# Routing and scattering of an expert layer's rows inside the attention before it, and results scattered by tags

## The chip, the cores and the metric

The kernel runs on one core of a Trainium2 chip. Its five engines are TensorE (PE), VectorE (DVE), ScalarE (ACT), GpSimd (POOL) and SyncE (SP); each works through its own list of instructions in order and waits for semaphores that others raise. DMAs are issued from SP's, ACT's and POOL's lists. The metric is the device time of one execution in microseconds; of several runs, the median counts.

## The reference

Two transformer blocks over 8 sequences of 256 tokens with 256 values (2,048 tokens). What matters here is the second block: an attention with 16 query heads and 4 key/value heads, causal, and behind it a mixture of experts.

```python
x = x + _L1_attn_ref(_layernorm(x), ...)
x = x + _L1_ffn_ref(_layernorm(x), ...)

# _L1_ffn_ref: 32 experts, 4 for each token, inner width 128, and a shared expert
logits = flat @ router_w.T
scores = jnp.sqrt(jax.nn.softplus(logits))
_, idx = jax.lax.top_k(scores + expert_bias, K)
topv = jnp.take_along_axis(scores, idx, axis=1)
topv = topv / (topv.sum(axis=-1, keepdims=True) + 1e-20)
probs = jnp.zeros((T, E), flat.dtype).at[jnp.arange(T)[:, None], idx].set(topv)
# for each expert: acc + p[:, None] * _clamped_swiglu(flat, wg, wu, wd)
out = out + _clamped_swiglu(flat, shared_gate_w, shared_up_w, shared_down_w)
```

## The kernel before

All engines' programs are written out by hand, with their waits. The stages follow each other: a front (projections of the first block), attention(0), a middle (output projection, the first block's expert choice, projections of the second block), attention(1), routing, shared expert, expert loop, combination.

**Attention.** `attention(n)` runs over 8 sequences b and 16 heads s. TensorE computes the scores twice: `pair` gives them to DVE, which takes the row maxima (L1423 in the second attention, six reduces a sequence), and `scores` gives them, with the maxima subtracted, to ACT for the exponential (L775). The maxima travel as two more rows of the stacked queries: DVE writes `neg`, TensorE turns it (`turn_maxima`, at head 8), ACT copies it to `negT` (L754, at head 9), and `stack_maxima` (L596, on POOL's list) sends two small DMAs into the rows of qs; TensorE waits for them at the start of the sequence (`neg_stacked`). In the second attention the stacked queries and keys come from DRAM by 12 DMAs for each 512 tokens that SP issues (`stack_middle`, L447 and L450). `values` multiplies four heads' probabilities with v; `turn_back` and `divide` (head 5 of the next sequence) give the normalized context, and DVE adds it to x (L1453).

Scores for ACT, maxima and turned values share a ring of three PSUM banks, `st_bank`. Its uses are listed in order in `RING_USES`; `wait_ring` makes TensorE wait until the use three places earlier is read.

**Routing**, all tokens at once after attention(1), with 16 tiles of 128 tokens: statistics (L1510 to L1517, ACT takes the root), normalized rows `xn4` (L1519), transposes (L1132) and copies (L1524), 64 matmul records for the logits (L1138), softplus as Exp and Ln and a square root on ACT (L813 to L817), the four best (L1542, L1545), one-hot `pick` (L1548) and its sum `chosen` (L1553), the weights `pk[1]` (L1556 to L1561), then with matmuls of ones and a triangle the rank of every row in its expert (L1147 to L1151), the table of blocks of 128 rows (L1565 to L1595), and the row numbers `slot` (L1581). Experts lie one behind the other, each rounded up to blocks, so that a row's place depends on the counts of all tokens.

**Scatter and loop.** POOL scatters each of 16 x 4 columns of rows into `rows_by_expert` (L647, 128 rows of 1 KB each). Meanwhile the shared expert runs in four chunks of 512 tokens (TensorE L1161, L1173; DVE L1602 to L1613; ACT L820). SP loads all experts' weights once attention(1) is over (L542), and the first blocks after the last scatter (L544). The loop works on 80 blocks here, four in each round, in a pipeline: TensorE turns the rows (L1193), computes gate and up (L1206), turns the hidden values (L1215), goes down (L1221); DVE clips (L1618), copies (L1637) and multiplies (L1624, L1630); ACT copies, takes tanh, copies the result (L837) and stores it to `results_by_expert` (L839).

**Combination.** When all results are stored (L1658), POOL gathers 64 times 128 rows by `slot` into eight buffers (L654), and DVE adds each, times its weight, to x (L1666). SP stores x, two tiles at a time (L559).

Both DRAM tables are filled with zeros before (L515, L516; 96 blocks and the last 32), by SP during attention(0).

## Time and profile before

| | us |
|---|---|
| runs (3) | 832.95, 834.35, 834.79; median 834.35 |
| profiled execution | 840.46 |
| its span, first to last instruction | 836.2 |
| mean granted TensorE clock | 0.832 |

| engine | busy us | share of the span |
|---|---|---|
| PE | 567.1 | 68% |
| DVE | 452.4 | 54% |
| ACT | 312.0 | 37% |
| POOL | 194.7 | 23% |

The page cuts the span into 40 slices of 20.9 us and gives the busy tenths of each. TensorE is at 7 to 9 in the first half and in the expert loop; between slice 20 and 27, and after the loop, it stands nearly still. Busy times are measured for each instruction; "idle before" is the time in which the engine stood in front of it, with who released it. "issue" as a releaser means that the profile shows nothing that was waited for. The granted clock is 1.00 at 2.4 GHz and 0.50 at 1.2 GHz.

### The profile page before, as it was taken

The numbers are of one execution on the slowest core, as the hardware profiler recorded it, in microseconds if no ns is written. First come the engines' busy times: TensorE is split into PE (matmuls) and PEld (weight loads), VectorE is DVE, ScalarE is ACT, GpSimd is POOL, SyncE is SP. The second block draws the span as 40 slices with busy tenths as digits, with TensorE's granted clock in tenths as the row PEclk, the third lists the DMA queues.
The fourth block names the chain that finished last, engine by engine and source line by source line (L and its number), as shares of the span: only waits on it lengthen the run. The fifth ranks groups of instructions, "written<-read, shape, count | busy, mean of one in ns | idle before, by whom it ended". The sixth has DMA issues, their size and how long they took to land.

```text
span 836.2 us, 13730 instructions
## 1 busy us (share of the span) xinstructions
PE 567.1 (68%) x4179; PEld 395.1 (47%) x4181; DVE 452.4 (54%) x1088; ACT 312.0 (37%) x755; POOL 194.7 (23%) x227
## 2 busy tenths in 40 slices
PE   5985797897977987999966235501799999960000
PEld 2652364454864556777746213200576767740000
DVE  4656487571688554666636595110455555543333
ACT  2441466566545523556650200000344455430000
POOL 2340000004110430000000017776000000007775
PEclk9995899899989897999995566755899999995555
DMA  6889949900000588000029202222344444423443
GB/s 197 224 264 215 204 152 408 351 2 3 1 2 0 148 255 184 3 4 3 3 71 421 114 6 94 106 101 103 101 136 134 137 135 134 138 84 118 129 140 114
DMA packets 61933, 107.40 MB, mean 128 GB/s; under 512 B 9333, under 2 KB 47421, under 8 KB 60477
## 3 DMA queue, kind: packets, MB, share of 16 engines
q1 hardware_dynamic: 43196, 79.23, 30.9%
q0 software_dynamic: 7168, 17.05, 6.5%
q10 hardware_dynamic: 11520, 10.49, 3.7%
q8 instruction: 29, 0.48, 0.2%
q14 instruction: 20, 0.16, 0.1%
HBM read 58.38 MB, written 47.97 MB: 127 GB/s over the span
## 4 chain that ended last, share of the span: by engine, by line
PE 48%; DVE 17%; issue 11%; POOL 8%; DMA 8%; ACT 4%; another core or an unknown queue 3%; SPq 1%; ACTq 0%; POOLq 0%; DVEq 0%
PE banks L1206 8%; POOL arena L654 6%; PE banks L1045 6%; PE banks L1221 5%; DMA arena<-negT 5%; PE banks L1007 4%; PE banks L884 4%; DVE mx L1420 3%; PE banks L1066 2%; PE banks L1193 2%; PE banks L1215 2%; PE banks L1048 2%; PE banks L890 2%; PE banks L952 2%
## 5 line engine op out<-in xcount | busy, mean ns | idle before, releaser
L775 ACT ACTIVATE arena<-banks 128x512 f32<-128x512 f32 (+1 forms) x256 | 130.8, 549 | 105.5 <-PE banks L1045 54.9
L1045 PE MATMUL banks<-arena 98*128 98x256 bf16 (+1 forms) x512 | 95.1, 274 | 30.5 <-DMA arena<-negT 22.7
L654 POOL DMA_INDIRECT arena<-results_by_expert,bpb x64 | 60.7, 948 | 187.9 <-DVE hold L1658 168.7
L1420 DVE TENSOR_REDUCE mx<-banks 128x4 f32<-128x1024 f32 x64 | 76.3, 1221 | 40.2 <-PE banks L1007 40.1
L1007 PE MATMUL banks<-arena 96*128 96x256 bf16 (+1 forms) x512 | 89.6, 282 | 5.2 <-DVE mx L1420 3.8
L647 POOL DMA_INDIRECT rows_by_expert<-arena,bpb x64 | 63.8, 997 | 99.1 <-DVE bpb L1581 79.9
L1206 PE MATMUL banks<-arena,attn_w 128*128 x320 | 83.8, 385 | 4.0 <-ACT attn_w L824 3.3
L1423 DVE TENSOR_REDUCE mx<-banks 128x4 f32<-128x1024 f32 (+1 forms) x48 | 58.3, 1223 | 40.1 <-PE banks L1011 39.4
L1045 PEld LDWEIGHTS banks<-arena 98*128 98x128 bf16 x512 | 47.3, 102 | 67.0 <-DMA arena<-negT 24.5
L601 POOL DMA_DIRECT2D arena<-negT x32 | 15.8, 497 | 230.0 <-ACT negT L754 230.0
L1007 PEld LDWEIGHTS banks<-arena 96*128 96x128 bf16 x512 | 53.1, 106 | 22.5 <-DVE mx L1420 7.3
L824 ACT ACTIVATE attn_w<-banks 128x256 f32<-128x256 f32 x80 | 30.6, 383 | 80.4 <-ACT attn_w L837 27.9
L1618 DVE TENSOR_SCALAR attn_w<-banks 128x256 f32<-128x256 f32 x80 | 34.0, 424 | 47.6 <-PE banks L1206 47.4
L1206 PEld LDWEIGHTS banks<-arena,attn_w 128*128 128x128 f32 x320 | 55.3, 193 | 9.1 <-issue 4.8
L1666 DVE SCALAR_TENSOR_TENSOR arena<-arena,pk 128x256 f32<-128x256 f32 x64 | 31.0, 485 | 51.4 <-DMA arena<-results_by_expert,bpb 47.0
L1221 PE MATMUL banks<-arena,attn_w 128*128 x160 | 51.5, 404 | 0.6
L1173 PE MATMUL banks<-arena 128*128 128x256 f32 x32 | 13.3, 588 | 51.2 <-DVE arena L1608 44.2
L1193 PE MATMUL banks<-ident,pvs 128*128 128x128 f32 x160 | 31.2, 279 | 18.2 <-DMA pvs<-rows_by_expert 18.2
L1011 PE MATMUL banks<-mask_s,identb 128*128 128x128 bf16 x256 | 43.1, 230 | 0.0
L1048 PE MATMUL banks<-mask_t,identb 128*128 128x128 bf16 x256 | 42.0, 224 | 0.0
L1066 PE MATMUL banks<-arena 128*17 128x256 f32 x512 | 36.3, 404 | 1.1 <-ACT pvs L763 1.1
L1173 PEld LDWEIGHTS banks<-arena 128*128 128x128 f32 x32 | 9.0, 295 | 56.3 <-DVE arena L1608 45.8
(197 smaller groups left out, 1024.3 us busy)
## 6 DMA issues: line engine op xcount, KB each, us to landing
arena<-parts_dram SPq DMA_DIRECT2D x72, 256.0 KB, 7.0
rows_by_expert<-zero SPq DMA_DIRECT2D x1, 12288.0 KB, 40.5
arena<-in SPq DMA_DIRECT2D x1, 12288.0 KB, 32.6
pvs<-rows_by_expert SPq DMA_DIRECT2D x80, 128.0 KB
results_by_expert<-attn_w ACTq DMA_DIRECT2D x80, 128.0 KB, 2.0
parts_dram<-arena SPq DMA_DIRECT2D x24, 384.0 KB, 3.2
results_by_expert<-zero SPq DMA_DIRECT2D x1, 4096.0 KB, 49.5
arena<-in SPq DMA_DIRECT2D x4, 512.0 KB, 6.6
```

The costliest lines, as they stand in the source:

```text
L647: pool.indirect_dma_start(xs, bass.IndirectOffsetOnAxis(ap=slot[:, t, k:k + 1], axis=0), xn4[:, t, :], None).then_inc(scattered, 16)
L654: pool.indirect_dma_start(yg[:, n % YG, :], None, ys, bass.IndirectOffsetOnAxis(ap=slot[:, t, k:k + 1], axis=0)).then_inc(gathered[n % YG] ...
L775: act.activation(pt[:, i % P_RING, 0:width], st_bank[RING_AT["s", b, s] % 3][:, 0:width], ACT.Exp, scale=HD ** -0.5).then_inc(exp_ready[n], 1)
L1007: ins = pe.matmul(dst[:, a * nk:(a + 1) * nk], q_rows(n, slice(0, STACK), h0 + a, b, qt * P, P), k_rows(n, slice(0, STACK), h0 + a, b, 0, ...
L1045: ins = pe.matmul(dst[:, at:at + SEQ - q0], keys, q_rows(n, slice(0, ROWS), s, b, q0, SEQ - q0), start=True, stop=(n == 0))
L1048: ins = pe.matmul(dst[:, at:at + P], identb[:, :], mask_t[:, :], start=False, stop=True)
L1066: ins = pe.matmul(pv_bank[rows, col:col + SEQ], vals, p[:, kt * SEQ:(kt + 1) * SEQ], start=(kt == 0), stop=(kt == QT - 1))
L1193: ins = pe.transpose(bank[p][:, k * P:(k + 1) * P], xb[:, q, k * P:(k + 1) * P], ident[:, :])
L1206: ins = pe.matmul(bank[2 + p][:, 0:2 * INNER], xbT[:, p, k, :], experts[:, bass.ds(e * EW + k * 2 * INNER, 2 * INNER)], start=(k == 0), st ...
L1221: pe.matmul(bank[6 + p][:, 0:D], hidT[:, p, :], experts[:, bass.ds(e * EW + 2 * KD * INNER, D)], start=True, stop=True).then_inc(y_ready, 1)
L1420: ins = dve.tensor_reduce(out, src.rearrange("p (q h k) -> p q h k", q=QT, k=nk), AX.X, ALU.max)
L1423: ins = dve.tensor_reduce(out, src.rearrange("p (h k) -> p h k", k=nk), AX.X, ALU.max)
```

## The change

**Layout.** `rows_by_expert` gets room for all 2,048 tokens in each expert (`EXPERTS * TOKENS` rows), so that a row's place is expert x 2,048 + rank and doesn't depend on later tokens. Rows become 260 values: 256 and four tags, expert x 16,384 + the number of the (token, choice) pair. Only the first 128 rows of each expert are cleared. A block may begin anywhere (`start_i`); an expert's last block is moved back to end with its rows, and rows that were done in the block before go to a trash area.

**Routing in the attention.** After `divide` of a sequence DVE takes its statistics; POOL takes the inverse root (`ALU.pow`) and ACT normalizes the rows at heads 8 and 10 of the next sequence; TensorE turns them at head 12 into a bank of the ring, and ACT copies. For five batches of sequences (3, 2, 1, 1, 1) logits are computed at head 14, ACT does Exp and Ln at head 15, POOL takes the square root as a power (`root`), DVE finds the best four and picks them at heads 3 and 8 of the second sequence after the batch, TensorE computes the ranks there at head 10 and DVE the row numbers at head 11. POOL scatters a batch's columns as soon as it has them, in between its small operations. Batches 3 and 4 end after the attention.

**Moved.** `stack_maxima(1, b)` goes from POOL to SP, behind `stack_middle(3)`. SP loads the experts in four parts, 5, 5 and 6 experts when their memory becomes free during the attention, and 16 when all slots are known; the shared expert's weights come after the last division. The weights `pk[1]` are computed after the expert loop.

**Expert loop.** ACT no longer stores. DVE finds for each block, from the tags, where its rows belong, and POOL scatters the result to the place of its (token, choice) pair in `results_by_token`. The combination then loads plain tiles with all four choices (16 loads of 512 KB, on SP and ACT) and adds them.

The diff, cut to its core:

```diff
+BATCHES = ((0, 3), (3, 2), (5, 1), (6, 1), (7, 1))
+NORMS, ROWS_AT, LOGITS_AT, SOFT_AT, SCORES_AT, TOP_AT, PICK_AT, RANKS_AT, SLOTS_AT = (8, 10), 12, 14, 15, 1, 3, 8, 10, 11
...
-            clear(xs, xs_cleared)
-            clear(ys[4 * FEWEST * P:BLOCKS * P, :], ys_cleared)
+            sp.dma_start(xs.rearrange("(e r) c -> r e c", e=EXPERTS)[0:P, :, :],
+                         zero[:, 0:XW].unsqueeze(1).broadcast_to([P, EXPERTS, XW])).then_inc(xs_cleared, 16)
...
             stack_middle(3)
+            for b in range(SEQS):
+                stack_maxima(b)
+                if b in (2, 4, 6):
+                    c = b // CS - 1
+                    sp.wait_ge(st_ready[1], b * HEADS)
+                    sp.wait_ge(neg_stacked[1], (b + 1) * 32)
+                    load_experts(c * STACK_C // 2 // EW, (c + 1) * STACK_C // 2 // EW)
+
+            sp.wait_ge(divided[1], SEQS * QT)
             sp.dma_start(wsh, wexp_in[:, EXPERTS, :]).then_inc(shared_loaded, 16)
+            sp.wait_ge(slots_ready, len(BATCHES))
+            load_experts(3 * STACK_C // 2 // EW, EXPERTS)
...
+            def scale_rows(b):
+                pool.wait_ge(rows_var, b + 1)
+                pool.tensor_tensor(rstd[:, at], var[:, at], mhalf[:, 0:QT], ALU.pow).then_inc(rows_root, 1)
+                pool.wait_ge(rows_root, b + 1)
+                pool.tensor_tensor(shift[:, at], nmean[:, at], rstd[:, at], ALU.mult).then_inc(rows_scaled, 1)
+            def root(j):
+                pool.wait_ge(soft_added, j + 1)
+                pool.tensor_tensor(sco[:, at, :], soft[:, 0:size * QT, :],
+                                   half[:, :].unsqueeze(1).broadcast_to([P, size * QT, EXPERTS]), ALU.pow
+                                   ).then_inc(root_ready, 1)
...
+            scale_rows(2)
+            root(0)
+            scale_rows(3)
+            scatter(0, 0, 8)
+            scale_rows(4)
+            scatter(0, 8, 17)
+            root(1)
...
+            scale_rows(7)
+            scatter(2, 0, 6)
+            root(4)
+            scatter(2, 6, 8)
+            scatter(3, 0, 8)
+            scatter(4, 0, 8)
+            with pool.Fori(0, block_trips(pool)) as i:
+                for j in range(4):
+                    pool.wait_ge(dest_ready, 4 * i + j + 1)
+                    pool.wait_ge(yb_copied, 4 * i + j + 1)
+                    pool.wait_ge(block_passed, 4 * i + j + 1)
+                    pool.tensor_tensor(spare[:, :], mhalf[:, 0:1], mhalf[:, 0:1], ALU.mult).then_inc(block_passed, 1)
+                    pool.indirect_dma_start(ys, bass.IndirectOffsetOnAxis(ap=goes[:, j:j + 1], axis=0),
+                                            yb[j], None).then_inc(y_stored[j], 16)
...
+            def soften(j):
+                act.activation(ex[:, 0:n, :], soft[:, 0:n, :], ACT.Exp).then_inc(soft_exp, 1)
+                act.wait_ge(soft_exp, j + 1)
+                act.activation(ln[:, 0:n, :], ex[:, 0:n, :], ACT.Ln, bias=1.0).then_inc(soft_ready, 1)
...
+            def turn_rows(b):
+                wait_ring(1, ("x", b, 0))
+                pe.wait_ge(rows_ready, (b + 1) * QT)
+                for k in range(KD):
+                    for t in range(QT):
+                        ins = pe.transpose(dst[:, at:at + P], xn4[:, b * QT + t, k * P:(k + 1) * P], ident[:, :])
...
+            def read_tags(b, q):
+                dve.wait_ge(xb_turned, b + 1)
+                dve.tensor_tensor(tag4[:, q, :], xb[:, q, D:XW], tagb[:, bass.ds(b, 1)].broadcast_to([P, TOPK]),
+                                  ALU.subtract).then_inc(dest_read, 1)
+            def find_rows(b, q, stored):
+                dve.wait_ge(dest_read, b + 1)
+                dve.tensor_reduce(near[:, q:q + 1], tag4[:, q, :], AX.X, ALU.min, apply_absolute_value=True
+                                  ).then_inc(dest_near, 1)
+                dve.wait_ge(dest_near, b + 1)
+                dve.scalar_tensor_tensor(out=goes[:, q:q + 1], in0=near[:, q:q + 1], scalar=float(TOKENS * TOPK - 1),
+                                         in1=pad[:, bass.ds(b, 1)], op0=ALU.min, op1=ALU.max).then_inc(dest_ready, 1)
```

## Rows read from the trace of the kernel before

**Rows 1.** Stretches: us, busy (x instructions) of PE, PEld, DVE, ACT, POOL, clock, DMA share, GB/s

```profile
331.00:345.60 14.60, 14.15 (x210) 11.11 (x202) 9.59 (x13) 8.48 (x22) 0.96 (x2) 1.00 0.01 3
...
436.00:499.00 63.00, 26.58 (x135) 21.86 (x136) 46.81 (x133) 7.24 (x8) 0.00 (x0) 0.58 0.47 200
...
583.00:750.00 167.00, 149.02 (x720) 110.64 (x720) 91.74 (x322) 76.84 (x240) 0.00 (x0) 0.97 0.41 126
```

**Rows 2.** Timeline (start us, us, operation): last division, first expert block

```profile
433.72 0.26 DVE L1438 RECIPROCAL rec<-banks 128x16 f32<-128x16 f32 x1 [7.17 <-PE banks L1083]
...
585.60 1.18 PE L1193 MATMUL banks<-ident,pvs 128*128 128x128 f32 x4 [18.22 <-DMA pvs<-rows_by_expert]
```

**Rows 3.** Groups of POOL by form: count, busy us, mean ns, idle before

```profile
L647 POOL DMA_INDIRECT rows_by_expert<-arena,bpb x64 | 63.8, 997 | 99.1 <-DVE bpb L1581 79.9 <-issue 19.2
...
L607 POOL TENSOR_TENSOR arena<-arena,bpb 128x4096 f32<-128x4096 f32 x1 | 8.9, 8918 | 0.0
L617 POOL TENSOR_TENSOR rstd<-var,mhalf 128x4 f32<-128x4 f32 x8 | 8.1, 1014 | 55.7 <-DVE nmean L1333 55.6
...
L619 POOL TENSOR_TENSOR shift<-nmean,rstd 128x4 f32<-128x4 f32 x8 | 1.6, 199 | 0.6
```

**Rows 4.** Timeline of the expert loop, DVE: blocks 4, 5 and 79

```profile
598.50 0.42 DVE L1618 TENSOR_SCALAR attn_w<-banks 128x256 f32<-128x256 f32 x1 [0.48 <-PE banks L1206]
...
599.36 0.29 DVE L1630 SCALAR_TENSOR_TENSOR attn_w<-attn_w 128x128 f32<-128x128 f32 x1
...
600.13 0.42 DVE L1618 TENSOR_SCALAR attn_w<-banks 128x256 f32<-128x256 f32 x1 [0.48 <-PE banks L1206]
...
743.67 0.42 DVE L1618 TENSOR_SCALAR attn_w<-banks 128x256 f32<-128x256 f32 x1 [0.98 <-PE banks L1206]
```

**Rows 5.** Timeline of the combination: first gather, last add

```profile
750.81 1.00 POOL L654 DMA_INDIRECT arena<-results_by_expert,bpb  x1 [168.73 <-DVE hold L1658]
...
832.48 0.48 DVE L1666 SCALAR_TENSOR_TENSOR arena<-arena,pk 128x256 f32<-128x256 f32 x1 [0.77 <-DMA arena<-results_by_expert,bpb]
```

**Rows 6.** DMA issues of the page: count, KB each, us to landing

```profile
arena<-in SPq DMA_DIRECT2D x1, 12288.0 KB, 32.6
...
results_by_expert<-zero SPq DMA_DIRECT2D x1, 4096.0 KB, 49.5
```

**Rows 7.** Waits between 115 and 188 us: us in total, times, longest

```profile
PE banks L1045 <- DMA arena<-negT: 6.8, 3, 3.1
```

**Rows 8.** Timeline, start of the second attention

```profile
315.10 1.05 POOL L601 DMA_DIRECT2D arena<-negT  x2 [9.98 <-ACT negT L754]
...
321.05 0.39 PE L1045 MATMUL banks<-arena 98*128 98x256 bf16 x1 [4.16 <-DMA arena<-negT]
...
324.78 0.59 SPq L450 DMA_DIRECT2D arena<-parts_dram  x1
```

**Rows 9.** Timeline, TensorE: turning values back, and the logits

```profile
433.02 1.09 PE L1083 MATMUL banks<-ident,pvs 128*128 128x128 f32 x8 [0.49 <-ACT pvs L763]
...
453.55 11.30 PE L1138 MATMUL banks<-wr,arena 128*128 128x32 f32 x64 [0.78 <-DVE arena L1524]
```

**Rows 10.** Timeline, ACT in the routing

```profile
466.34 0.63 ACT L813 ACTIVATE arena<-arena 128x512 f32<-128x512 f32 x1 [22.23 <-DVE arena L1529]
466.98 1.28 ACT L815 ACT_TABLE_LOAD   x1
```

**Rows 11.** Timeline, DVE in the routing

```profile
478.50 3.62 DVE L1553 TENSOR_REDUCE products<-arena 128x512 bf16<-128x2048 f32 x1
...
492.11 0.19 DVE L1574 TENSOR_TENSOR wd<-wd 128x32 f32<-128x32 f32 x1
```

**Rows 12.** Timeline, DVE in the shared expert: chunks 1, 2 and 3

```profile
516.83 0.69 DVE L1602 TENSOR_SCALAR arena<-banks 128x512 f32<-128x512 f32 x1 [3.94 <-PE banks L1161]
...
526.41 0.69 DVE L1602 TENSOR_SCALAR arena<-banks 128x512 f32<-128x512 f32 x1 [4.06 <-PE banks L1161]
...
560.80 0.69 DVE L1602 TENSOR_SCALAR arena<-banks 128x512 f32<-128x512 f32 x1 [21.71 <-remote]
```

More of the change, by code:

```diff
@@ L361, in two_block_kernel @@
         xs_cleared = sem("xs_cleared")
[L362 to L363 removed]
+        ones_placed, last_ones = sem("ones_placed"), sem("last_ones")
         qkv_loaded = sem("qkv_loaded")
@@ L538, in _, with stack_maxima, load_experts @@
             stack_middle(3)
+            def stack_maxima(b):
+                sp.wait_ge(negT_copied[1], b + 1)
+                for half in range(2):
+                    rows = slice(STACK + half, STACK + half + 1)
+                    dst = qs[1][b // CS][rows, :, b % CS * SEQ:(b % CS + 1) * SEQ]
+                    sp.dma_start(dst, negT[half * HEADS:(half + 1) * HEADS, :]).then_inc(neg_stacked[1], 16)
+            def load_experts(first, last):
+                sp.dma_start(experts[:, first * EW:last * EW].rearrange("p (e w) -> p e w", w=EW),
+                             wexp_in[:, first:last, :]).then_inc(experts_loaded, 16)
@@ new lines, in _ @@
+            then(dve.tensor_copy(rows[:, :], bank[7][:, 0:EXPERTS]))
+            then(dve.tensor_scalar(cnti[0][:, :], rows[:, :], float(P - 1), None, ALU.add))
+            then(dve.tensor_scalar(cnti[1][:, :], cnti[0][:, :], P.bit_length() - 1, None, ALU.logical_shift_right))
+            then(dve.tensor_copy(blocks[:, :], cnti[1][:, :]))
+            then(dve.tensor_tensor(after, iota32[:, :].unsqueeze(2).broadcast_to(ee),
+                                   iota32[:, :].unsqueeze(1).broadcast_to(ee), ALU.is_ge))
@@ new lines, in _ @@
+            then(dve.tensor_tensor(after, after, blocks[:, :].unsqueeze(1).broadcast_to(ee), ALU.mult))
+            then(dve.tensor_reduce(upto[:, :], after, AX.X, ALU.add))
+            start, expert, fresh, end_row, nth, lead, total, raw, live = (vec[:, i:i + 1] for i in range(9))
+            then(dve.tensor_scalar(over[:, :], upto[:, :], iota_p[:, 0:1], None, ALU.is_le))
+            dve.tensor_reduce(raw, over[:, :], AX.X, ALU.add)
+            then(dve.tensor_tensor(these[:, :], over[:, :], blocks[:, :], ALU.mult))
@@ new lines, in _ @@
+            then(dve.tensor_reduce(nth, these[:, :], AX.X, ALU.add))
+            then(dve.tensor_scalar(expert, raw, float(EXPERTS - 1), None, ALU.min))
+            then(dve.tensor_scalar(over[:, :], iota32[:, :], expert, None, ALU.is_equal))
+            then(dve.tensor_tensor(these[:, :], over[:, :], rows[:, :], ALU.mult))
+            then(dve.tensor_reduce(total, these[:, :], AX.X, ALU.add))
+            then(dve.tensor_tensor(nth, iota_p[:, 0:1], nth, ALU.subtract))
+            then(dve.tensor_scalar(nth, nth, float(P), None, ALU.mult))
@@ new lines, in _ @@
+            dve.wait_ge(spread_ready, 1)
+            starts, owners, froms, ends = (bank[6][:, i * P:i * P + BLOCKS] for i in range(4))
+            dve.tensor_copy(start_i[:, :], starts[0:1, :])
+            dve.tensor_copy(eb_i[:, :], owners[0:1, :])
+            dve.tensor_scalar(tagb, owners, TAG, None, ALU.mult)
+            then(dve.tensor_scalar(valid, froms, iota_p[:, 0:1], None, ALU.is_le))
+            then(dve.scalar_tensor_tensor(out=valid, in0=ends, scalar=iota_p[:, 0:1], in1=valid,
+                                          op0=ALU.is_gt, op1=ALU.mult))
```

615 lines of the change are left out of this document (383 added, 232 removed).

## Prediction, made before the changed kernel ran

> **What bounds the kernel now.** I read the stages first. A sequence of the second attention lasts 14.6 us, and TensorE is busy for 14.15 of them, DVE 9.6, ACT 8.5 [rows 1]. In the routing stage behind it DVE works 46.8 of 63 us and every other engine waits [rows 1]. The timeline says where the chain breaks: the last sequence is divided at 433.72, and the first transpose of an expert block starts at 585.60, 151.9 us later [rows 2]. Most of that is 64 scatters, one after the other on POOL: 0.997 us of descriptor making and 0.30 us before the next [rows 3]. The expert loop then takes 167 us [rows 1]; two blocks in its straight part start 1.63 us apart [rows 4]. From 750.81 to 836.2, 85.4 us, POOL gathers 64 times and each add of 0.48 us waits for its gather [rows 5].
>
> The profiled execution took 840.46 us for a span of 836.2, and the median of the runs is 834.35, 6.1 lower. I sum on 840.46 and take 6.1 off at the end. A measurement of this kernel can tell about 0.2% from no change.
>
> **Part 1, clearing.** Before, 96 and 32 blocks of 128 rows are cleared (16.8 MB) in the first attention, the second part landing after 49.5 us [rows 6]. TensorE waits there three times for the row maxima's small DMA, 6.8 us together [rows 7]. After, 32 x 128 rows of 1,040 bytes (4.3 MB) remain. The first wait also has the load of x in front of it and stays. Gain 5, bounds 0 and 6.8.
>
> **Part 2, the maxima move from POOL's queue to SP's.** stack_maxima(0) of the second layer now stands on SP behind stack_middle(3). Before, POOL issued it at 315.10 and TensorE went on at 321.05; SP's last stack DMA goes out at 324.78 for 0.59 us [rows 8]. So the maxima go out from 325.4. If they landed at once, the attention and all behind it would start 5 us later; if they need the 4.9 us that POOL's needed behind its 1.05 of issue [rows 8], 10 later. I take +10, since they now share a queue with the transfers in front of them. From then on SP is free, and the later maxima have six heads' time to land. wsh, which was loaded at this point, moves behind divided[1]; its use is 25 us later. The expert loads of 2 MB each (about 5 us at 12.6 MB in 32.6 [rows 6]) start with a sequence, eight heads before the next maxima, so I cost them at nothing; without that distance, 5 us each.
>
> **Part 3, routing inside the attention.** TensorE has no room, so what it gets is paid in full. Four transposes for each of seven sequences at 1.09/8 = 0.136 us are 3.8. Logits: 14 tiles x 4 records at 11.30/64 = 0.177 are 9.9 [rows 9], but TensorE was cold there, with 0.58 of its clock over the routing stage [rows 1], and the attention runs at 1.00 [rows 1]; at full speed 5, I take 6. The ranks of three batches are 28 bf16 matmuls, each under such a transpose; I take 2. Together 12. ACT: for four batches Exp and Ln, and each change of function costs a table load. The trace shows one of 1.28 before Ln although Exp had just run [rows 10]; the way back to softmax costs another. With the operations that is some 3.3 us in which no head gets its exponential. The ring of three score banks hides about two heads, 1.8 us; 1.5 remain, four times: 6. DVE gets about 4 us a sequence, and the batch of three sequences far more: its reduce alone is 6/16 of 3.62 [rows 11]. 9.6 + 4 fits into 14.6, the large batch doesn't: 4 us. Each new use of a ring bank waits for a copy or read that stands in its engine's order (turn_rows for ACT, logits and ranks for DVE), and the next scores queue behind it on TensorE: 4 us. Sum +26; bounds 12 (TensorE's work alone) and 45 (no stall hidden).
>
> The Trainium skill has a rule against my table loads: "ScalarE: Activation LUTs", section "Table sets: the hidden batching unit", says that exp and ln share a set, so one load serves both. By it, 6 of the 26 us fall away. The trace disagrees, with its 1.28 us load between Exp and Ln [rows 10].
>
> **The new POOL operation.** The root is a power with exponent 0.5 on POOL, on 192, 128, 64, 64 and 64 values of each partition. The trace has a power on 4 values, 1.014 us, a multiply on 4, 0.199, and an add of 4,096 in 8.9, 2.2 ns each [rows 3]. If the extra 0.81 is a start cost, each root is 1 to 1.5 us; if it is paid for each value (0.20), they are 39, 26 and 3 x 13. I take 1 to 3 us, by the slope that POOL's own long operation shows, and keep the other end as a rival.
>
> **Part 4, from the last division to the first block.** The chain, from 433.72: divide 2.1; statistics 1.3; POOL power and shift 1.2; two normalizations 1.2; transposes, copy, logits 2.9 at the half clock; read 0.4; Exp, Ln and their two loads 3.2; root 1.5 (POOL passes six scatters before it, 7.6 us, in the same time); top four and picks 1.9; ranks 1.5; slots 1. That is 18. Tables: three operations over 1,024 values at 1.2 and some 25 of 0.19 [rows 11] plus a matmul step, 10.5, to 28.5. The shared expert needs TensorE, ACT and DVE; its chunks came 9.6 us apart [rows 12], so four and their drain are 42: 71. Beside it: of 64 scatters some 46 fit before the attention's end (slots of the first batch are ready 60 us before it, at 1.3 us each), the rest end at about 38; the last expert load, 6.3 MB, takes 16.4 and ends at about 36. Both hide under the shared expert; if that were gone they would set 40. I take 72 against 151.9: -80, bounds -60 and -97 (the shared expert at the full clock).
>
> **Part 5, expert loop.** Removed: ACT's store, off the path. Added on DVE: three small operations for each block, 0.19 each [rows 11] with waits 0.6 to 0.8. DVE needed 1.15 of each 1.63 (from L1618's start to L1630's end [rows 4]) and now needs 1.75 to 1.95. TensorE's mean is 1.94 (145.17 us for 75 blocks [rows 4]), because each fourth block loads registers for the next ones. So DVE just becomes equal: +10, bounds 0 and 38. POOL's new scatter with its small multiply takes 1.3 + 0.3 to 0.6, under 1.94; ACT waits for it four blocks later, so it is free unless it is slower than the pace.
>
> **Part 6, the end.** One last scatter 1.7 and its landing 2. Sixteen loads of 512 KB at 386 GB/s [rows 6]: the first four are there after 7.5. The weights' six DVE operations, about 5.5, hide under this wait. 64 adds at 0.48 and 0.05 for the dependence are 34, the last store 3.2 (832.96 to 836.2 [rows 5]). From the old starting point of 85.4 us: 1.7 + 7.5 + 34 + 3.2 = 46. Gain 40, bounds 36 and 43.
>
> Sum: -5 + 10 + 26 - 80 + 10 - 40 = -79; 840.46 - 79 = 761.5, on the median's level 755.
>
> **The rivals.** (a) *The loop is paced by DVE or POOL.* For: DVE's margin is gone on paper. Against: TensorE's 0.3 us a block above the straight part's 1.63 are room for both. At 2.4 us a block, +38 instead of +10: 783. The Trainium skill ("SBUF — State Buffer", section "SBUF: two separate sides") speaks for it: a DVE operation with two SBUF inputs and a GpSimd operation that reads SBUF keep each other out. No row here settles that.
> (b) *The power costs by the value; this ends slower.* DVE waits for root(0) at head 3 of the fifth sequence, and TensorE behind it: 37 us; root(1) 24, root(2) 12, the last two 12 each on the chain of part 4. That is +97: 852. It decides from 79/512 = 0.155 us a value. For: nothing in the trace separates start from slope. Against: no other POOL row grows so. Between the ends, 0.05 a value gives about 780.
> (c) *The unexplained waits come along.* While POOL scattered, DVE stood 21.71 us for a semaphore whose sender no row shows [rows 12]. If that belongs to the scatters and not to the place, 46 scatters in the attention bring 30 us (785), and in the loop more still (above 850). Against: beside the gathers, as dense on POOL, an add waits 0.77 us and for a DMA that is named [rows 5].
> (d) *Better.* The shared expert at the full clock (-12) and the attention at TensorE's work alone (-14): 729.
>
> **How the numbers follow.** Forecast 0.56 (735 to 775), (a) 0.12, (b) 0.12, of which 0.05 are slower than before, (c) 0.10, 0.02 of it slower, (d) 0.10. The predicted time is 755. The range 728 to 802 leaves out the upper ends of (b) and (c), some 0.12, and half of (d). Faster 0.92, same 0.01, slower 0.07.
>
> **What would show it.** Part 2: between the last stack DMA's issue and the second layer's first scores lie 1 to 7 us, spent waiting for negT. Part 3: sequences of 16 to 19 us, table loads of 1.28 in four of them, TensorE waiting behind them; POOL's line of the power with 64, 128 and 192 values gives (b) directly. Part 4: 72 us from the last reciprocal to the first block, the shared expert last. Part 5: distance of L1618's successor, and what it waits for. Part 6: DVE adds 0.53 apart without waits. The prediction is wrong where one of these is off by over 15 us.

## The result, and the profile after

The changed kernel takes 865.9 us (median of 4 runs, 862.6 to 869.3) against 834.0 of the kernel before in the same comparison: a ratio of 1.037, 95% interval 1.033 to 1.040. It is slower; 755 with a range of 728 to 802 had been forecast. Its profiled execution took 863.06 us for a span of 861.3. Ratios leave out executions more than 1.5% above the fastest of the same kernel, which below concerns one of e11's four (770.0 us).

Five marks of both traces cut the span as the prediction cut it (us; the kernel before in [rows 2, 5, 8], the changed one by the same lines of code):

| stretch | before | forecast change | after | change found |
|---|---|---|---|---|
| start to first scores of layer 2 | 321.1 | +5 | 322.5 | +1.5 |
| from there to the last division | 112.7 | +26 | 226.2 | +113.5 |
| last division to first expert block | 151.9 | -80 | 92.7 | -59.2 |
| first block to last scatter (before: first gather) | 165.2 | +10 | 175.6 | +10.4 |
| from there to the end | 85.4 | -40 | 44.4 | -41.0 |

Three of the five came as forecast. The second attention is 87 us off, the routing behind it 21 us.

POOL's groups by form in the changed kernel (count, busy us, mean ns, idle before). L738 is the new root, L696 and L729 are powers on four and on two values:

```profile
L738 POOL TENSOR_TENSOR arena<-arena,half 128x64 f32<-128x64 f32 x3 | 31.7, 10580 | 9.9 <-DVE arena L1658 9.9
L738 POOL TENSOR_TENSOR arena<-arena,half 128x192 f32<-128x192 f32 x1 | 31.0, 31007 | 11.2 <-DVE arena L1658 11.2
L738 POOL TENSOR_TENSOR arena<-arena,half 128x128 f32<-128x128 f32 x1 | 20.8, 20808 | 6.9 <-DVE arena L1658 6.9
...
L696 POOL TENSOR_TENSOR rstd<-var,mhalf 128x4 f32<-128x4 f32 x8 | 8.1, 1013 | 55.6 <-DVE nmean L1535 55.6
...
L729 POOL TENSOR_TENSOR rstd<-var,mhalf 128x2 f32<-128x2 f32 x8 | 6.0, 752 | 96.3 <-DVE nmean L1645 96.3
```

From 64 to 192 values the time grows by (31.007 - 10.580) / 128 = 0.160 us a value, from two to four by 0.13; the start costs some 0.4. The five roots take 83.6 us. Two groups of the page say who pays:

```profile
L738 POOL TENSOR_TENSOR arena<-arena,half 128x64 f32<-128x64 f32 (+2 forms) x5 | 83.6, 16711 | 28.0 <-DVE arena L1658 28.0
...
L1665 DVE TENSOR_TENSOR arena<-arena,ebb 128x64 f32<-128x64 f32 (+2 forms) x5 | 1.3, 265 | 76.5 <-POOL arena L738 76.5
```

DVE's first operation of the top four stands 76.5 us for them, and behind it in DVE's order wait the reduces for the row maxima and the next division, so TensorE stops too. The chain of waits between 425 and 620 us (start, us, what) shows a second guest:

```profile
441.18 7.12 another core or an unknown queue
...
459.10 4.32 issue
...
473.61 20.82 POOL arena L738
...
507.95 3.76 another core or an unknown queue
...
514.55 10.58 POOL arena L738
...
535.89 8.72 another core or an unknown queue
...
547.45 10.59 POOL arena L738
...
567.78 10.59 POOL arena L738
...
596.21 7.82 another core or an unknown queue
```

The first root, 31.02 us from 390.83, stands ahead of this window. The first three roots are 62.4 us and lie in the attention (the fourth begins 1.3 us before its end). The four pieces up to 545 us that name no sender (one is called issue) are 23.9. Together they are 86.3 us, beside 87 that the attention is off; that they meet so closely is partly chance, since e13 puts the nameless waits at 17.5 there and the rest of part 3 was forecast too low, as is said below. The last two roots, 21.2, are the 21 of the routing. In the timeline a piece without a name looks like this (start, us, engine, line, operation, idle before):

```profile
537.86 0.22 PE L1206 MATMUL banks<-mask_t,identb 128*128 128x128 bf16 x1
543.90 0.23 DVE L1651 COPY arena<-banks 128x64 f32<-128x64 f32 x1 [10.78 <-remote]
...
544.63 0.49 ACT L924 ACTIVATE arena<-banks 128x384 f32<-128x384 f32 x1 [8.27 <-remote]
```

TensorE's records end at 538.08, but DVE and ACT go on only 5.8 and 6.5 us later, both in the same microsecond. In this kernel every line that waits so for over 1 us reads what TensorE has written, so I read "remote" as a signal of TensorE that arrived late. POOL was issuing scatters one behind the other just then, from 531.8 to 542.9.

The end is as forecast (chain of waits, then a line of the timeline): the last scatter's landing, 7.40 us for the first loads, then adds 0.49 us apart, ten in 4.92 us, where each waited for its gather before [rows 5]:

```profile
816.95 2.43 DMA results_by_token<-attn_w,goes
819.80 7.40 DMA arena<-results_by_token
```

```profile
827.31 4.92 DVE L1948 SCALAR_TENSOR_TENSOR arena<-arena,pk 128x256 f32<-128x256 f32 x10 [9.94 <-DMA arena<-results_by_token]
```

### The profile page after: what moved, and what is told of

Same layout as the page of the kernel before. It is cut to its first block, busy times and chain, and to the rows that moved or that the text cites. A ratio compares the mean times of both kernels' runs of the same rounds, so it can differ in the third digit from the quotient of the medians.

```text
span 861.3 us, 14750 instructions
## 1 busy us (share of the span) xinstructions
PE 587.9 (68%) x4230; PEld 398.0 (46%) x4231; DVE 473.5 (55%) x1381; ACT 323.3 (38%) x790; POOL 312.7 (36%) x332
## 4 chain that ended last, share of the span: by engine, by line
PE 48%; DVE 18%; POOL 12%; issue 5%; DMA 5%; ACT 4%; another core or an unknown queue 3%; SPq 3%; ACTq 0%; DVEq 0%; POOLq 0%
POOL arena L738 10%; PE banks L1408 8%; PE banks L1423 6%; PE banks L1203 5%; PE banks L1159 4%; PE banks L1036 4%; DVE arena L1948 4%; DMA arena<-negT 3%; PE banks L1224 3%; DVE mx L1622 2%; PE banks L1395 2%; PE banks L1417 2%; PE banks L1042 2%; PE banks L1104 1%
## 5 line engine op out<-in xcount | busy, mean ns | idle before, releaser
L1203 PE MATMUL banks<-arena 98*128 98x256 bf16 (+1 forms) x512 | 100.9, 283 | 106.6 <-DVE arena L1721 38.6
L1203 PEld LDWEIGHTS banks<-arena 98*128 98x128 bf16 x512 | 49.4, 106 | 143.6 <-DVE arena L1721 42.2
L738 POOL TENSOR_TENSOR arena<-arena,half 128x64 f32<-128x64 f32 (+2 forms) x5 | 83.6, 16711 | 28.0 <-DVE arena L1658 28.0
L783 POOL DMA_INDIRECT results_by_token<-attn_w,goes x80 | 78.8, 985 | 37.1 <-issue 35.1
L1408 PE MATMUL banks<-arena,attn_w 128*128 x320 | 83.7, 385 | 0.7 <-issue 0.6
L981 ACT ACTIVATE attn_w<-attn_w 128x128 f32<-128x128 f32 x80 | 24.8, 310 | 97.6 <-DVE attn_w L1873 94.9
L1423 PE MATMUL banks<-arena,attn_w 128*128 x160 | 55.0, 426 | 1.3 <-issue 0.2
L680 POOL DMA_DIRECT2D arena<-negT x16 | 8.0, 502 | 116.8 <-ACT negT L882 116.8
L1206 PE MATMUL banks<-mask_t,identb 128*128 128x128 bf16 x256 | 47.5, 242 | 0.2 <-issue 0.2
L782 POOL TENSOR_TENSOR spare<-mhalf 128x1 f32<-128x1 f32 x80 | 16.9, 212 | 83.6 <-DVE goes L1908 64.0
L1665 DVE TENSOR_TENSOR arena<-arena,ebb 128x64 f32<-128x64 f32 (+2 forms) x5 | 1.3, 265 | 76.5 <-POOL arena L738 76.5
L729 POOL TENSOR_TENSOR rstd<-var,mhalf 128x2 f32<-128x2 f32 x8 | 6.0, 752 | 96.3 <-DVE nmean L1645 96.3
```

The source lines that it names most:

```text
L738: pool.tensor_tensor(sco[:, at, :], soft[:, 0:size * QT, :], half[:, :].unsqueeze(1).broadcast_to([P, size * QT, EXPERTS]), ALU.pow).then_ ...
L783: pool.indirect_dma_start(ys, bass.IndirectOffsetOnAxis(ap=goes[:, j:j + 1], axis=0), yb[j], None).then_inc(y_stored[j], 16)
L1203: ins = pe.matmul(dst[:, at:at + SEQ - q0], keys, q_rows(n, slice(0, ROWS), s, b, q0, SEQ - q0), start=True, stop=(n == 0))
L1206: ins = pe.matmul(dst[:, at:at + P], identb[:, :], mask_t[:, :], start=False, stop=True)
L1408: ins = pe.matmul(bank[2 + p][:, 0:2 * INNER], xbT[:, p, k, :], experts[:, bass.ds(e * EW + k * 2 * INNER, 2 * INNER)], start=(k == 0), st ...
L1423: pe.matmul(bank[6 + p][:, 0:D], hidT[:, p, :], experts[:, bass.ds(e * EW + 2 * KD * INNER, D)], start=True, stop=True).then_inc(y_ready, 1)
```

## Experiments

Two theories stood at the outset. A: POOL's power is paid by the value, and everything lost is DVE's stop for it. C: the waits without a sender come with the scatters and cost as much or more. The kernels e1 to e4 were measured beside each other on one chip, e5 to e8 on a second one, e9 to e11, e12 to e15 and e16 to e18 on three more, each time beside the kernel before. That becomes important below. Ratios are against the kernel before.

**e1, the power replaced by a multiply.** It leaves the root out, so its result is another one; it is there for the time alone.

```diff
-  half[:, :].unsqueeze(1).broadcast_to([P, size * QT, EXPERTS]), ALU.pow
+  half[:, :].unsqueeze(1).broadcast_to([P, size * QT, EXPERTS]), ALU.mult
```

> The changed kernel with one word changed: POOL multiplies by 0.5 where it took the power 0.5. It leaves out the square root of the scores (and so may choose other experts; the count of blocks may move by one or two). Theory A (POOL's power on 128 to 192 values is what costs): the five operations fall from 83.6 us to under 3 together, DVE's 76.5 us of waiting for them goes, and the time is 866 - 76 = 790, or 780 to 800. Theory C (the waits with no sender that stand beside the dense scatters cost more than the power): the five operations get short, but sequences stay above 20 us, and the time is over 820. If the waits with no sender belong to the scatters, they stay in the attention: 20 us or more of waits marked remote or issue while POOL scatters.

Measured: 792.0 us, ratio 0.949 (0.943 to 0.954). POOL's root by form, same columns as above:

```profile
L738 POOL TENSOR_TENSOR arena<-arena,half 128x64 f32<-128x64 f32 x3 | 0.9, 314 | 9.3 <-DVE arena L1658 9.3
...
L738 POOL TENSOR_TENSOR arena<-arena,half 128x192 f32<-128x192 f32 x1 | 0.6, 587 | 11.2 <-DVE arena L1658 11.2
```

Same engine, place, tiles and waits, and 31.0 us became 0.59. The number of expert blocks stayed at 80. One operation is worth 865.9 - 792.0 = 74 us (73 by the ratios), close to DVE's 76.5 us of waiting. Theory A holds for its amount; but the chain of waits still has 34.1 us in seven pieces without a name (one of them called issue) between 409 and 533 us, so C isn't refuted.

**e2, the root on ACT.** The result is the changed kernel's; the root is ACT's Sqrt, the top four move from head 3 to head 5.

```diff
-  pool.tensor_tensor(sco[:, at, :], soft[:, 0:size * QT, :], half..., ALU.pow).then_inc(root_ready, 1)
+  act.activation(sco[:, at, :], soft[:, 0:size * QT, :], ACT.Sqrt).then_inc(root_ready, 1)
```

> The same result as the changed kernel, with the root taken on ACT (Sqrt, 0.25 to 0.4 us for each batch) after head 2 and the top four moved from head 3 to head 5. Theory A: about 76 us less than the changed kernel for the power, and 4 x 2.6 us of table loads more (Sqrt and back to Exp): 866 - 76 + 10 = 800, or 785 to 810. If the loads are hidden by the ring of score banks, it equals e1 within 5 us. Theory C: over 820.

Measured: 815.4 us, ratio 0.976 (0.970 to 0.981): faster than the kernel before, 23 us above e1 where 10 were expected. ACT's timeline around the first batch shows the price, four table loads:

```profile
391.74 1.28 ACT L899 ACT_TABLE_LOAD   x1
...
393.41 1.28 ACT L917 ACT_TABLE_LOAD   x1
...
395.98 1.28 ACT L906 ACT_TABLE_LOAD   x1
...
397.65 1.28 ACT L917 ACT_TABLE_LOAD   x1
```

They are to Ln, back to Exp, to Sqrt and back. Four batches with 5.1 us of loads are 20 us where e1 and the changed kernel have 10, and the attention is 10.1 us longer than e1's (182.0 against 171.9). That the loads alone make these 10.1 us isn't shown: the top four moved too, and in e11 two loads less in each batch shorten the attention by 1.0 us. Another 10.6 of the 23 lie between the last division and the first block, where two more loads and a wait of 13 us without a sender stand, and 4.0 ahead of the second attention, where the two texts are the same.

**e3, all scatters behind the attention; e4, plain copies at their old places.** Both on e2. In e4 POOL issues, where e2 scatters, `pool.dma_start(copies[...], xn4[:, t, :])` of the same rows, and the scatters stand late as in e3.

```diff
-  scale_rows(3); scatter(0, 0, 8); scale_rows(4); scatter(0, 8, 17); ...
+  for b in range(SEQS): scale_rows(b)
+  for j in range(len(BATCHES)): scatter(j, 0, BATCHES[j][1] * QT * TOPK)
```

> e2 with all 64 scatters behind POOL's last shift, so none runs inside the attention. If the waits with no sender come from the scatters, they leave the attention (300 to 550) altogether, sequences take 15 to 18 us each, and the attention ends 20 to 30 us earlier than in e2; if they belong to the place in the program, they stay there. Behind the attention the 64 scatters at 1.3 us are 83 us, about 35 us more than what stands there in e2 and partly beside the shared expert: last division to first block about 90 to 110 us. Net against e2: between -10 and +30 us.

> e3, and at the places where e2 scatters, POOL issues a plain DMA of the same 128 rows of 1,040 bytes into a tensor of its own that nobody reads (64 more, added work). If the waits with no sender come from the bytes or the packets in the DMA queues, they are back in the attention as in e2 (20 us or more). If they come from what POOL does for an indirect DMA, the attention is as in e3 within 5 us.

Measured: 821.3 and 815.4 us. Waits of e2 from 320 to 500 us (engine, line, us in total, times, longest):

```profile
DVE mx L1623 <- remote: 20.3, 3, 8.8
...
ACT arena L917 <- remote: 19.6, 4, 8.0
```

POOL's timeline of e4 shows eight plain copies in 4.36 us:

```profile
409.83 4.36 POOL L749 DMA_DIRECT2D copies_of_rows<-arena  x8 [8.77 <-DVE bpb L1717]
```

In e3 and e4 no wait of that stretch is named remote, and from first scores to last division they need 155.6 and 154.6 us where e2 needs 182.0. Behind the attention, where the scatters now stand, the waits are back. e3 from 480 to 610 us:

```profile
DVE arena L1840 <- remote: 21.3, 1, 21.3
...
DVE arena L1851 <- remote: 12.0, 2, 7.8
...
DVE wd L1794 <- remote: 12.0, 1, 12.0
...
DVE start_i L1825 <- remote: 11.0, 1, 11.0
```

So last division to first block took 122.9 us, outside the expected 90 to 110: these waits are longer there. On one chip the waits went where the indirect scatters went, and plain copies of the same rows, issued still more densely (0.54 us each), brought none in the attention. It isn't the bytes. C holds: it is a second cost of its own.

**e5, the maxima ahead of the last chunk's stack.** On e2.

```diff
   stack_middle(2)
+  stack_maxima(0)
   stack_middle(3)
-  stack_maxima(0)
```

> e2 with the first row maxima of the second layer put on SP ahead of the last chunk's stack DMAs instead of behind them. Part 2's price is 9.1 us by the two traces (first scores 5.39 us behind the last stack DMA's issue where they were 3.73 ahead of it before): 9 us less than e2, 815 to 806, and the first scores 3 us or more ahead of the last stack DMA. Rival: the first scores then wait for something else that ends at the same time (the last chunk's data or TensorE's own work), and the gain is under 3 us.

Measured: 811.4 us, 4.0 below e2's, ratios 0.968 (0.964 to 0.973) and 0.976 (0.970 to 0.981), hardly apart. The first scores of the changed kernel and of e5, each beside its last stack DMA, in two timelines:

```profile
317.12 0.59 SPq L497 DMA_DIRECT2D arena<-parts_dram  x1
...
322.51 0.40 PE L1203 MATMUL banks<-arena 98*128 98x256 bf16 x1 [15.60 <-DMA arena<-negT]
```

```profile
314.10 0.39 PE L1203 MATMUL banks<-arena 98*128 98x256 bf16 x1 [7.63 <-DMA arena<-negT]
...
316.82 0.59 SPq L497 DMA_DIRECT2D arena<-parts_dram  x1
```

5.4 us behind became 2.7 ahead: 8.1 us at this place. Behind it e5's attention and routing are longer than e2's by several us, on another chip, and swallow half of it; why wasn't tested. On its own chip, e6, e7 and e8 have their first scores at 320.7 to 323.8.

**e6, a pause behind each scatter.** On e2.

```diff
   pool.indirect_dma_start(xs, ..., xn4[:, t, :], None).then_inc(scattered, 16)
+  pool.tensor_tensor(zero[:, 0:D], zero[:, 0:D], zero[:, 0:D], ALU.mult).then_inc(filled, 1)
+  pool.wait_ge(filled, ...)
```

> e2 with a POOL multiply of 256 values behind each of the 64 scatters into the experts' rows, so that they come 1.9 to 2.1 us apart instead of 1.27, which is the distance in the expert loop, where no such waits stand. If the distance decides, the waits with no sender fall from some 60 us in e2 (320 to 560) to under 10, although the scatters last longer, and the time is below e2 by 5 to 20 us. If each scatter holds the others up wherever it stands, they stay as they are or grow, and the time is above e2 by 10 us or more.

Measured: 787.6 us, ratio 0.939 (0.937 to 0.941), 28 below e2 and 24 below e5, its neighbour on the same chip. POOL's timeline shows the new distance, 1.94 us:

```profile
431.26 1.01 POOL L740 DMA_INDIRECT rows_by_expert<-arena,bpb  x1 [0.28 <-POOL zero L742]
432.30 0.62 POOL L742 TENSOR_TENSOR zero<-zero 128x256 f32<-128x256 f32 x1
433.20 1.01 POOL L740 DMA_INDIRECT rows_by_expert<-arena,bpb  x1 [0.28 <-POOL zero L742]
```

No wait between 320 and 620 us is named remote any more, while e5, e7 and e8, on the same chip, have 43 us or more of them over DVE and ACT, from 320 to 500 us alone. The scatters got slower and the kernel faster.

**e7, every scatter of the expert loop issued twice.** On e2; the second one goes to a tensor that nobody reads.

```diff
   pool.indirect_dma_start(ys, ..., yb[j], None).then_inc(y_stored[j], 16)
+  pool.indirect_dma_start(copies, ..., yb[j], None).then_inc(y_stored[j], 16)
```

> e2 with each scatter of the expert loop issued twice, the second time into a tensor of its own that nobody reads. POOL then needs 2.7 to 2.9 us a block instead of 2.0, so the loop gets 55 to 70 us longer for that alone. If back-to-back scatters hold up TensorE's signals everywhere, the loop's DVE or ACT show waits with no sender of several us. If the loop is safe from them for another reason (its instructions, its place), there are none, and each wait names POOL or the scatter's landing.

Measured: 928.2 us (one run), 113 above e2. In the loop, which had shown none, there are now such waits (640 to 800 us):

```profile
ACT attn_w L977 <- remote: 18.7, 8, 6.0
...
DVE attn_w L1874 <- remote: 10.4, 5, 4.1
...
DVE attn_w L1893 <- remote: 5.5, 5, 1.8
```

So the loop isn't immune. In e2 it has one scatter in 2 us, behind waits and a small multiply; in e7 a second one follows directly. Which of the two differences, the number or the missing gap, brings the waits this run can't say.

**e8, one operation moved into a gap.** On e2: the reduce of find_rows now stands between the two operations of hidden.

```diff
   dve.scalar_tensor_tensor(out=gu[:, p, 1, :], ...).then_inc(hid_step, 1)
+  near_rows(*find)
   dve.wait_ge(hid_step, b + 1)
```

> e2 with one DVE operation of the expert loop moved: the reduce that finds a row's tag stands between the two operations of the hidden layer, where DVE waits 0.23 us for its own result, and no longer ahead of the last one, which waited 0.26 us for it. If DVE paces the loop (2.03 us a block in both changed kernels, 1.92 before), about 0.15 to 0.3 us a block fall away until TensorE paces it: 8 to 10 us less than e2, and waits for TensorE come back on DVE. If the loop is paced by POOL or TensorE now, it stays within 3 us.

Measured: 807.6 us, 7.8 below e2, ratio 0.965 (0.962 to 0.967). In the loop of the changed kernel DVE's clip waits 3.8 us for TensorE in all 80 blocks and ACT's tanh 94.9 for DVE; in e8, from 650 to 740 us alone, DVE waits 4.1 for TensorE again, and first block to last scatter take 167.6 us where e2 needs 173.8:

```profile
L981 ACT ACTIVATE attn_w<-attn_w 128x128 f32<-128x128 f32 x80 | 24.8, 310 | 97.6 <-DVE attn_w L1873 94.9
...
L1873 DVE TENSOR_SCALAR attn_w<-banks 128x256 f32<-128x256 f32 x80 | 34.0, 424 | 3.8 <-PE banks L1408 3.6
```

```profile
L1871 DVE TENSOR_SCALAR attn_w<-banks 128x256 f32<-128x256 f32 x45 | 19.1, 424 | 6.0 <-PE banks L1406 4.1 <-issue 0.9
```

So DVE paced the loop, and one of its two stops for its own results was worth 6.2 of the 10.4 us of part 5.

**e9, e14, e15: which part of the pause matters?** On e2: the multiply cut to one value; the multiply without a wait for it; a wait alone, in front of each scatter, for a semaphore that is long there.

```diff
+  pool.wait_ge(slots_ready, j + 1)                                                  (e15)
   pool.indirect_dma_start(xs, ..., xn4[:, t, :], None).then_inc(scattered, 16)
+  pool.tensor_tensor(zero[:, 0:1], zero[:, 0:1], zero[:, 0:1], ALU.mult)...          (e9)
+  pool.wait_ge(filled, ...)                                                         (e9)
+  pool.tensor_tensor(pads[:, ...], zero[:, 0:1], zero[:, 0:1], ALU.mult)            (e14)
```

> e6 with the multiply behind each scatter cut from 256 values to 1 (0.2 us), so that the scatters come 1.55 to 1.65 us apart. If any operation of POOL between two scatters lets TensorE's signals through, the waits with no sender stay under 5 us in all and the time is 5 to 20 us below e6, 768 to 783, since the scatters behind the attention end sooner. If it takes the distance of 2 us, they are back in part: 10 us or more of them, and the time is above e6.

> e2 with a multiply of 1 value behind each scatter that nothing waits for, so the scatters come 1.3 to 1.5 us apart. If an operation of POOL between two scatters is enough, no waits without a sender and 772, as e9. If the stop for its result is what counts, they are there as in e2, and the time is 805 to 820.

> e2 with a wait in front of each scatter for a semaphore that has long reached its value (slots_ready), and no operation; it costs POOL under 0.1 us. If a look at a semaphore is enough to let the others through, 772 as e9; if not, 810 to 820 and the same waits without a sender as e2.

Measured: 771.9, 769.4 and 769.0 us, ratios 0.927, 0.922 and 0.923, and none of them shows a wait named remote between 320 and 620 us. In e15 the scatters even come 1.27 us apart, as in e2. Taken alone this would say that any of the three is a cure. It says less, since neither group had e2 itself beside them, and e18 takes the conclusion away.

**e18, e7 with a bare wait ahead of the second scatter.** On another chip than e7.

```diff
+  pool.wait_ge(xs_cleared, 16)
   pool.indirect_dma_start(copies, ..., yb[j], None).then_inc(y_stored[j], 16)
```

> e7 (two scatters for each block of the expert loop) with a bare wait in front of the second one, which had none. If a scatter that follows on another without any wait is what holds TensorE's signals up, the waits with no sender go from the loop (some 35 us between 640 and 800 in e7), and the loop is paced by POOL alone at 2.7 to 2.9 us a block: 928 falls to 870 to 890. If they come from the number of scatters, it stays at 928.

Measured: 815.1 us (one run), 113 below e7 and far below what was expected. First block to last scatter takes 221.8 us, 2.77 a block, which is POOL's own time for two scatters and the multiply; in e7 it took 280.4. So of e7's 107 us above e2's loop some 48 are POOL's own time. But the gain is not all in the loop. The 64 scatters ahead of the loop are e2's, 1.27 us apart and with no wait, and yet from first scores to last division e18 needs 154.7 us where e7, with the same text there, needs 186.5, and no wait is named remote. An edit in the loop can't well do that. The chip may: all kernels of the first two groups but e6 have these waits, and no kernel of the last three, whatever is in front of its scatters. That is an inference and no test, since no edited kernel ran on two chips, and in the third and fourth group none without a pause or a wait ran at all. The kernel before gives a hint but doesn't decide it: it was 836.8 and 838.2 us in the first two groups and 832.5, 833.0 and 832.3 in the others, but also 834.0 in the first comparison, where its trace has such waits.

**e13, the changed kernel with e9's pause,** and its power as it is.

```diff
   pool.indirect_dma_start(xs, ..., xn4[:, t, :], None).then_inc(scattered, 16)
+  pool.tensor_tensor(zero[:, 0:1], zero[:, 0:1], zero[:, 0:1], ALU.mult).then_inc(filled, 1)
+  pool.wait_ge(filled, ...)
```

> The changed kernel with POOL's power left as it is, and only the short pause of e9 behind each scatter. It gives the share of the waits with no sender alone: they fall from some 30 to 40 us to none. e9 gave 43 us on e2; here the five powers already part the scatters into shorter bursts, so 25 to 40 us less than 866: 826 to 841. If the power covers these waits (DVE waits for it anyway), less than 15 us.

Measured: 842.6 us, ratio 1.012 (1.008 to 1.016), no wait named remote. For what it shows it is the same whether the pause or the chip took those waits away: without them the changed kernel is still 1.2% slower than the kernel before. On the same chip e14 and e15, which have the root on ACT, are 73 us below it; so the power is what keeps it slow, and e1's 74 us are found a second time, now with the root kept. The two ratios put the waits without a sender at 1.037 - 1.012, some 21 us, and the traces show 17.5 of it in the attention (208.7 against 226.2).

**e16, the kernel before with a bare wait ahead of each scatter.**

```diff
+  pool.wait_ge(slots_ready, 1)
   pool.indirect_dma_start(xs, ..., xn4[:, t, :], None).then_inc(scattered, 16)
```

> The kernel before, with a wait for a semaphore that has long reached its value in front of each of its 64 scatters, as in e15. The waits with no sender in its routing stage (21.7 us on DVE's L1602 alone) go. The first block there waits for the last scatter, 3.2 us ahead of it, which no wait of this kind delayed; so the time falls by 0 to 5 us. If the scatters too were slowed by these waits, 10 to 20 us less.

Measured: 831.7 us, ratio 0.999 (0.997 to 1.001). The 21.71 us of [rows 12] are gone, whether by the edit or by the chip, on which e18's scatters had no such waits without any edit. So the ratio doesn't tell what these waits cost. The traces do: last division to first block takes 151.9 us in e16 and 151.9 in the kernel before, with and without them. The first block stands behind the last scatter there, and the stops lay beside that.

**e10, e11, e12, e17: the edits together.** e10 is e2 with e5, e6 and e8. e11 adds the scores in one go on ACT:

```diff
+  act.activation(lg[:, 0:n, :], src, ACT.Exp).then_inc(logits_read, 1)
+  act.activation(soft[:, 0:n, :], lg[:, 0:n, :], ACT.Ln, bias=1.0).then_inc(soft_exp, 1)
+  act.activation(lg[:, 0:n, :], soft[:, 0:n, :], ACT.Ln).then_inc(soft_ready, 1)
+  act.activation(sco[:, at, :], lg[:, 0:n, :], ACT.Exp, scale=0.5).then_inc(root_ready, 1)
```

e12 has the pause of e9 and e17 the bare wait of e15 in place of e6's.

> e2 with the three edits of e5 (maxima earlier), e6 (paced scatters) and e8 (reduce in the gap) together. If they work in different places they add up: 787.6 less what e5 and e8 gave by their traces, 9 for the first scores and 8 in the loop: 770, or 766 to 776. If one of them only moved a wait, it stays above 780.

> e10 with the scores wholly on ACT, in one go: Exp of the logits from PSUM, Ln of 1 plus that, Ln, and Exp of half of it in place of the Sqrt. Two table loads of 1.28 us for each batch instead of four, and DVE's three operations on the logits are gone. 4 batches in the attention and one behind it, 2.6 us each for the loads and 1 for waits on DVE: 10 to 18 us less than e10, 752 to 762. If the loads are hidden by the ring of score banks or by the paced scatters, under 4 us.

> e11 with the short pause of e9 (multiply of 1 value) in place of the long one. Behind the attention the last scatters end 64 x 0.45 us sooner in all, of which about 9 us showed in e9 against e6 between the attention's end and the first block: 761 - 9 = 752, or 745 to 757. If the shared expert already sets the end there, under 3 us.

> e12 with the bare wait of e15 in place of the short multiply: the scatters come 1.27 us apart instead of 1.49. Behind the attention some 30 scatters are left, so 0 to 7 us less than e12: 741 to 748.

Measured: 769.4, 761.4, 748.0 and 747.3 us; ratios 0.924 (0.921 to 0.926), 0.911 (0.908 to 0.914), 0.899 (0.895 to 0.902) and 0.897 (0.895 to 0.900). By the ratios e10 is 43 us below e2, but the chips differ; beside e9, which has the short pause alone and ran on the same chip, it is 2.6 us below, as its longer pause takes back most of what e5's and e8's edits give. e11's scores in one go are worth 8 us (10 by the ratios), of which the attention shows 1.0, the shorter pause some 10 by the ratios, and e12 and e17 are equal. Each sets its own place: e17 has its first scores at 316.6 us, first block to last scatter 163.9, against 322.5 and 175.6. The idea of the change is sound: with the root elsewhere and the other edits it is 10% faster than the kernel before. Whether e12 or e17 would keep that on a chip of the first two groups wasn't tried; of the pauses only e6's, which e10 and e11 have, was seen to hold there.

## Why the prediction was wrong

The step that failed is the paragraph on the new POOL operation: "I take 1 to 3 us, by the slope that POOL's own long operation shows". It measured 31.0, 20.8 and three times 10.6 us. That slope, 2.2 ns a value [rows 3], is that of an add. For a power the only row was 1.014 us for four values, beside 0.199 for a multiply of four in the same group of rows, and the extra 0.81 had two readings, a start or 0.20 a value. The second was right, with 0.16 a value and about 0.4 of start (0.752 us for two values and 1.013 for four, in the profile after). Rival (b) had put that at 852 us and its point of decision at 0.155; it got a chance of 0.12. e1 is the proof: the same operation as a multiply gives back 74 us, and e13 beside e14 gives 73 again. What weighed the chance was the argument that no other POOL row grows so; but the other rows were other functions, and one row can't separate a start from a slope. With a bound of 39 us for the one operation that stops two engines, the two ends were cases of equal standing, and the range should have reached 852.

Rival (c), the waits without a sender, came too, and on top of (b): 23.9 us of them on the chain in the attention, 7.8 beside the shared expert, and some 21 in the time by e13. It had been priced at 30 us, so it was nearly right in size; that they would also come in the loop was not so. Its reason against (none beside the gathers) was void: while POOL gathers, TensorE does nothing whose signal could be late. e3 and e4 show that the indirect scatters bring them. The range was drawn from one cause at a time; both came.

The other steps, point by point:

- Part 1, clearing, -5: the exponentials of the first attention ran from 80.6 to 203.2 us and now from 81.2 to 196.7, 7.1 less, a little over the upper bound.
- Part 2, maxima on SP, +10: the first scores moved from 3.7 us ahead of the last stack DMA to 5.4 behind it, 9.1; e5 gives back 8.1. Right. The first stretch of the table grew by 1.5 only, as the 7.1 of part 1 lie in it too.
- Part 3, routing in the attention, +26 (12 to 45): e15, with neither power nor remote waits, needs 156.6 us from first scores to last division against 112.7: +44. With two loads in a batch, as forecast, e12 and e17 still need 154.3 and 151.3: +42 and +39 against 26. Inside the bounds, but the term was too small by 13 us or more. Part of it is TensorE's own work, forecast at 12: its busy time in this stretch is 125.9 us in e17 and 132.2 in e15 against 108.0, at a granted clock of 0.94 and 0.89 against 0.97. The other part is time in which it stands, 25 us against 5 and forecast at 14.
- Part 4, -80: 92.7 us, of which 21.2 are the last two roots; without them 71.5 against the forecast 72, although a wait of 7.8 without a name is in it. In e15 it is 69.6. Right.
- Part 5, the loop, +10: 10.4, and e8 shows that it is DVE, as said. Rival (a)'s 2.4 us a block and +38 didn't come.
- Part 6, -40: -41.0. Right, with some luck: its sum names the last landing, 2 us, and leaves it out (it took 2.4), and its 34 us of adds took 31.4.

Taken together: e15's 769 us is the forecast kernel with its root on ACT, against 755 predicted; the 18 us that part 3 had too little stand against some 7 that the other parts gained beyond their forecast. The case was lost in one line of POOL, and the second cause was priced only by itself.

The table loads came as [rows 10] had said, 1.28 us between Exp and Ln in every batch of every kernel, against the one table set that the Trainium skill names for both ("ScalarE: Activation LUTs", "Table sets: the hidden batching unit"). Where the two differ, the measurement counts.

## What to carry to other kernels

Take the price of an operation from a row of the same function at two sizes; where only one size is there, start and slope are two forecasts, and the one that stops another engine decides the range. Before an operation moves onto an engine in the middle of a pipelined stretch, name what stands behind its reader: here DVE's maxima and TensorE's scores paid for each microsecond of POOL. And look at waits that have no sender as a cost that belongs to a neighbour (here indirect scatters back to back), test by moving the neighbour, and have the unedited kernel measured on the same chip each time.

## What was not expected of the hardware

POOL's power costs 0.16 us for each value of a partition (31.0 us for 128x192), where its multiply of the same tile takes 0.59.

Indirect scatters of 128 rows, issued 1.27 us apart, went together with stops of DVE and ACT for TensorE's signals, up to 21 us at a time (e3); where the lateness can be read against TensorE's records, it was 5.8 and 6.5 us. Plain DMAs of the same rows 0.54 us apart had none beside them (e4), nor had indirect ones 1.94 us apart with a multiply between (e6). Two scatters a block in the expert loop made it 280 us long instead of 174 (e7); without such waits, in e18, it took 222. These stops were seen on the chips of the first comparison and of e1 to e8, and on those of e9 to e18 not once, also where the scatters stood as in e2 (e18). What in POOL's issue does it, whether and why it depends on the chip, and whether a bare wait ahead of a scatter helps where it occurs is open: no kernel without a pause was run beside e9, e14 and e15.
